# First norm's affine rows folded into the up weights, its token copy and the weight rounding moved to GpSimd, and all orders laid anew, in a one-core sandwich block

## The reference, cut to what matters

```
ln0(v)  = (v - mean) / sqrt(var + 1e-5)
ln(v)   = ln0(v) * g + b                      # the affine rows ln_g, ln_b
mlp(v)  = gelu(v @ w1 + b1) @ w2 + b2         # 128 -> 512 -> 128

# attention-like part, on u = ln0(x)
n  = ln(u)
W1, W2 = mlp_h1(n), mlp_h2(n)
t  = tril(W1 @ W2^T) @ n                      # per sequence of 256 tokens
x1 = u + ln(gelu(t))
x  = x + ln0(u + mlp_fm(ln(x1)))

# feed-forward part, on y = ln0(x), ternary weights, scales per output
h  = silu(y @ w1) * (y @ w2)
h  = gelu(gelu(h @ a) @ b)                    # 512 -> 512 -> 512
x  = x + ln0(h @ w3)
```

## Time and profile before

| | us |
|---|---|
| median of 3 runs | 365.95 |
| profiled execution: span from first to last instruction | 362.6 |
| median less this span | 3.35 |
| TensorE busy, share | 350.1, 97% |
| its weight loads busy | 289.2, 80% |
| VectorE | 319.9, 88% |
| ScalarE | 305.2, 84% |
| GpSimd | 147.2, 41% |

### The profile page before, as it was taken

How to read it: one execution, slowest core, us unless ns; L and a number is a source line. 1 busy time by engine, 2 the same in 40 slices (tenths; PEclk the granted TensorE clock), 3 DMA queues, 4 the chain that set the end, 5 groups by cost and what they waited for, 6 DMA issues and landing times.

```text
span 362.6 us, 6039 instructions
## 1 busy us (share of the span) xinstructions
PE 350.1 (97%) x1788; PEld 289.2 (80%) x1788; DVE 319.9 (88%) x954; ACT 305.2 (84%) x552; POOL 147.2 (41%) x213
## 2 busy tenths in 40 slices
PE   6989999999999999999999999999999999999993
PEld 5867687778888888888888888888888887788992
DVE  5889999999999999889989989998969998886936
ACT  5999999997779979988599888897799569959892
POOL 4168842860546052504750286003920174044411
PEclk9999999999999999999999999999999999999998
DMA  7507020000000000000010001000000001001111
GB/s 233 174 14 245 4 60 1 1 2 1 3 0 0 2 0 2 17 13 2 1 29 3 0 0 33 0 1 2 1 0 2 0 2 31 0 2 29 32 30 33
DMA packets 8804, 9.08 MB, mean 25 GB/s; under 512 B 577, under 2 KB 6722, under 8 KB 8770
## 3 DMA queue, kind: packets, MB, share of 16 engines
q1 hardware_dynamic: 8226, 8.41, 7.7%
q10 hardware_dynamic: 544, 0.26, 0.2%
HBM read 6.57 MB, written 2.10 MB: 24 GB/s over the span
## 4 chain that ended last, share of the span: by engine, by line
PE 67%; ACT 13%; DVE 10%; issue 5%; DMA 2%; POOL 1%; SPq 1%; POOLq 0%; DVEq 0%; ACTq 0%
PE bank L1224 8%; PE bank L1226 8%; PE bank L1240 6%; PE bank L1241 6%; PE bank L1123 4%; PE bank L1104 4%; PE bank L1108 4%; PE bank L1105 4%; PE bank L1120 4%; PE bank L1121 4%; PE bank L1206 4%; PE bank L1209 4%; ACT h_hidden_hi L510 3%; PE bank L1046 2%; ACT bank L515 2%
## 5 line engine op out<-in xcount | busy, mean ns | idle before, releaser
L715 DVE TENSOR_TENSOR ffn_gate_lo<-bank,ffn_gate_hi 128x512 fp32r<-128x512 f32 (+1 forms) x72 | 44.1, 626 | 6.0 <-ACT bank L584 4.9
L510 ACT ACTIVATE h_hidden_hi<-bank,cols 128x512 fp32r<-128x512 f32 x64 | 46.1, 760 | 3.5 <-PE bank L1108 3.2
L515 ACT ACTIVATE bank<-bank,cols 128x512 f32<-128x512 f32 x64 | 45.1, 739 | 0.3
L715 DVE TENSOR_TENSOR h_hidden_lo<-bank,h_hidden_hi 128x512 fp32r<-128x512 f32 x64 | 43.0, 681 | 2.5 <-ACT bank L515 2.5
L584 ACT ACTIVATE bank<-bank,cols 128x512 f32<-128x512 f32 (+1 forms) x72 | 43.7, 620 | 0.7
L1224 PE MATMUL bank<-ffn_gate_hi,ffn_w_hi 128*128 128x512 f32 (+1 forms) x108 | 40.5, 381 | 0.2 <-DVE ffn_gate_lo L715 0.2
L1226 PE MATMUL bank<-ffn_gate_lo,ffn_w_hi 128*128 128x512 f32 (+1 forms) x108 | 39.3, 370 | 0.2 <-DVE ffn_gate_lo L715 0.2
L578 ACT ACTIVATE ffn_h_hi<-bank,cols 128x512 fp32r<-128x512 f32 (+1 forms) x36 | 23.0, 646 | 13.5 <-PE bank L1226 8.3
L578 ACT ACTIVATE ffn_gate_hi<-bank,cols 128x512 fp32r<-128x512 f32 (+1 forms) x36 | 23.2, 647 | 10.6 <-PE bank L1226 8.3
L364 POOL TENSOR_TENSOR XR<-X,ln_x_r 128x512 f32<-128x512 f32 x8 | 8.3, 1042 | 53.6 <-DVE bank L861 53.4
L715 DVE TENSOR_TENSOR ffn_h_lo<-bank,ffn_h_hi 128x512 fp32r<-128x512 f32 (+1 forms) x36 | 22.0, 626 | 8.0 <-ACT bank L584 7.8
(11 more groups left out here) (164 smaller groups left out, 1132.3 us busy)
## 6 DMA issues: line engine op xcount, KB each, us to landing
raw<-ffn_w SPq DMA_DIRECT2D x5, 512.0 KB, 3.9
out<-X SPq DMA_DIRECT2D x7, 256.0 KB, 2.3
raw<-attn_w SPq DMA_DIRECT2D x6, 256.0 KB, 4.9
X<-x SPq DMA_DIRECT2D x3, 256.0 KB, 5.6
raw<-ffn_w SPq DMA_DIRECT2D x1, 256.0 KB, 3.2
X<-x ACTq DMA_DIRECT2D x1, 128.0 KB, 2.5
X<-x SPq DMA_DIRECT2D x1, 128.0 KB, 2.3
out<-X SPq DMA_DIRECT2D x1, 128.0 KB, 1.8
```

The source lines that it names most:

```text
L510: nc.scalar.activation(dst, bank(f"{L}u{j}", c)[:, :], ACT.Gelu, bias=bias_of(L, j)).then_inc(*hi[L].done(c, j))
L515: nc.scalar.activation(u[:, :], u[:, :], ACT.Gelu, bias=bias_of(L, j)).then_inc(*act2[L].done(c, j))
L715: return nc.vector.tensor_tensor(dst, whole, high.bitcast(f32), ALU.subtract)
```

## The change

1. `n_first` and `n_second` become one `n_norm(c)` on VectorE: four tensor_scalar, NF = (x - mean) * scale, with two per-partition scalars and no row. It waits for `n_lo(c - 1)` and for the scale.
2. The up weights of h1 and h2 are rounded with the scale column g, as those of fm were; `h_bias_product` (eight one-column matmuls with the column b, into a new bank group hb) and `h_bias_add` give the biases of h1 and h2. TensorE's transposes take the NF without the affine rows.
3. For the tokens GpSimd applies the rows in place, after the transposes: `n_gain(c)` and `n_shift(c)`, one 128x512 tensor_tensor each with a broadcast row; `n_high` waits for them, and `n_low` as before for `n_high`.
4. `ffn_w_hi` moves from ScalarE to GpSimd, as a tensor_copy into fp32r.
5. The bias b2 of fm comes by a DMA of one column into fm_b2, in place of a row, a tiny matmul and a copy; `fm_evict(0)` waits for it. SP issues it after chunk 2's x. SP waits for `h_b` too ahead of feed-forward piece 0, since the bias product reads raw.
6. TURNS and the lists of all four compute engines are laid anew. On TensorE `down_mm("h2", 3, 3)`, `down_mm("fm", 0, 1)` and `up_mm("fm", 3, 1)` move ahead of the branch.

```diff
-            def n_first(c):
+            def n_norm(c):
                 if c:
-                    dve.wait_ge(*nT.at(c - 1))
                     dve.wait_ge(*n_lo.at(c - 1))
-                else:
-                    dve.wait_ge(*rows_ready.at(0))
-                dve.wait_ge(*x_stats.at(c, 1))
-                for t in range(T):
-                    last = nc.vector.scalar_tensor_tensor(NF[:, t, :], X[:, c * T + t, :], mv("x", c)[:, t, 0:1], bc[:, R_G, :], ALU.subtract, ALU.mult)
-                last.then_inc(*n_v.done(c))
-
-            def n_second(c):
-                dve.wait_ge(*n_v.at(c))
                 dve.wait_ge(*x_scale.at(c, 1))
                 for t in range(T):
-                    nc.vector.scalar_tensor_tensor(NF[:, t, :], NF[:, t, :], x_s[:, t:t + 1], bc[:, R_B, :],
-                                                   ALU.mult, ALU.add).then_inc(*n_v_ready.done(c, t))
+                    nc.vector.tensor_scalar(NF[:, t, :], X[:, c * T + t, :], mv("x", c)[:, t, 0:1], x_s[:, t:t + 1],
+                                            ALU.subtract, ALU.mult).then_inc(*n_v_ready.done(c, t))
...
+            def n_gain(c):
+                if c == 0:
+                    pool.wait_ge(*rows_ready.at(0))
+                pool.wait_ge(*nT.at(c))
+                nc.gpsimd.tensor_tensor(NF[:, :, :], NF[:, :, :], row(R_G), ALU.mult).then_inc(*n_made.done(c, 0))
+
+            def n_shift(c):
+                pool.wait_ge(*n_made.at(c, 0))
+                nc.gpsimd.tensor_tensor(NF[:, :, :], NF[:, :, :], row(R_B), ALU.add).then_inc(*n_made.done(c, 1))
...
+            def ffn_w_hi(i):
+                c0, c1, at = F_PIECES[i]
+                pool.wait_ge(ffn_in[i], 16)
+                nc.gpsimd.tensor_copy(Fw[0][:, c0:c1], raw[:, at:at + c1 - c0]).then_inc(*ffn_hi.done(0, i))
...
             def attn_w_hi(i):
-                if i == PIECE["fmu"]:
+                if i in UP_PIECES:
...
+            def h_bias_product():
+                bank_free("hb", 0)
+                pe.wait_ge(cols_in, 16)
+                for L in ("h1", "h2"):
+                    pe.wait_ge(attn_in[PIECE[f"{L}u"]], 16)
+                    for j in range(J):
+                        w = ATTN[f"{L}u"] + j * P
+                        last = nc.tensor.matmul(bank("hb", 0)[:, C_B1[L] + j:C_B1[L] + j + 1], raw[:, w:w + P], cols[:, C_B:C_B + 1],
+                                                start=True, stop=True)
+                last.then_inc(*h_b.done(0))
...
+            def h_bias_add():
+                dve.wait_ge(*h_b.at(0))
+                nc.vector.tensor_tensor(h_bias[:, :], bank("hb", 0)[:, 0:2 * J], cols[:, 0:2 * J], ALU.add).then_inc(*h_b_added.done(0))
...
-            sp.dma_start(b2_row, rows[2:3, :]).then_inc(b2_in, 16)
             x_piece(1, 1, 2)
             for i in (3, 4, 5):
                 attn_piece(i)
             x_piece(2, 2, 3)
+            sp.dma_start(fm_b2[:, :], rows[2:3, :].rearrange("o d -> d o")).then_inc(b2_in, 16)
             for i in (0, 1):
                 sp.wait_ge(*attn_lo.at(0, 2 * i + 1))
+                if i == 0:
+                    sp.wait_ge(*h_b.at(0))
                 ffn_piece(i)
```

The first steps of GpSimd's order, before and after:

```diff
-            x_s_(0); n_low(0); x_s_(1); x_s_(2); lo_block(0); lo_block(1); x_r(0); xr_scale(0); lo_block(2); xr_b(0)
-            lo_block(3); n_low(1); t_r(0); x_r(1); lo_block(4); lo_block(5); x1_r(0); lo_block(6); lo_block(7); x_s_(3)
-            lo_block(8); n_low(2); t_r(1); xr_scale(1); xr_b(1); lo_block(9); o_r(0); x_r(2); x1_r(1); lo_block(10); y_r(0)
+            x_s_(0); n_gain(0); n_shift(0); n_low(0); ffn_w_hi(0); x_s_(1); lo_block(0); x_s_(2); x_r(0); lo_block(1)
+            xr_scale(0); n_gain(1); ffn_w_hi(1); ffn_w_hi(2); n_shift(1); lo_block(2); lo_block(3); n_low(1); x_r(1)
+            xr_b(0); t_r(0); lo_block(4); lo_block(5); ffn_w_hi(3); n_gain(2); x1_r(0); ffn_w_hi(4); x_s_(3); n_shift(2)
+            lo_block(6); lo_block(7); lo_block(8); ffn_w_hi(5); n_low(2); n_gain(3); lo_block(9); t_r(1); xr_scale(1)
+            xr_b(1); x_s_(4); o_r(0); lo_block(10); x1_r(1); n_shift(3); o_shift_(0); y_centre(0); y_r(0); y_scale(0)
```

And of VectorE's after, from chunk 2's pass to chunk 3's:

```diff
+            fm_bias_add(); up_lo("h1", 3, 1); x_st(4); t_st(0); n_norm(2); t_ag(0); up_lo("h2", 1, 1); t_gain(0)
+            nT_low(2); x1_sum(0); up_lo("h2", 2, 1); x1_st(0); x1_ag(0); up_lo("h2", 3, 1); down_lo("h1", 1)
+            up_lo("h1", 0, 2); x_ag(4); up_lo("h1", 1, 2); m_norm(0); down_lo("h2", 1); up_lo("h1", 2, 2)
+            up_lo("h2", 0, 2); mT_low(0); score_mask(0, 1); score_mask(1, 1); up_lo("h2", 1, 2); gate_constants()
+            score_lo(0, 1); score_lo(1, 1); up_lo("fm", 0, 0); up_lo("h2", 2, 2); up_lo("h1", 3, 2); up_lo("fm", 1, 0)
+            n_norm(3); up_lo("fm", 2, 0); t_st(1); up_lo("fm", 3, 0); t_ag(1); nT_low(3); t_gain(1); down_lo("h1", 2)
```

More of the change, by code:

```diff
@@ L88, in sandwich_block @@
     PIECE = {name: i for i, name in enumerate(ATTN)}
+    UP_PIECES = [PIECE[name] for name in ("h1u", "h2u", "fmu")]
     F_W1, F_W2, F_W3 = 0, DI, 2 * DI
@@ L430, in x_end @@
                 nc.gpsimd.tensor_tensor(xc(c), xc(c), FN[:, :, :], ALU.add).then_inc(*x_out.done(c))
-            x_s_(0); n_low(0); x_s_(1); x_s_(2); lo_block(0); lo_block(1); x_r(0); xr_scale(0); lo_block(2); xr_b(0)
-            lo_block(3); n_low(1); t_r(0); x_r(1); lo_block(4); lo_block(5); x1_r(0); lo_block(6); lo_block(7); x_s_(3)
-            lo_block(8); n_low(2); t_r(1); xr_scale(1); xr_b(1); lo_block(9); o_r(0); x_r(2); x1_r(1); lo_block(10); y_r(0)
-            y_centre(0); y_scale(0); o_shift_(0); n_low(3); x_s_(4); xr_scale(2); xr_b(2); o_r(1); t_r(2); x_r(3); x1_r(2)
@@ L436, in _ @@
-            y_r(1); y_centre(1); y_scale(1); o_shift_(1); x_s_(5); n_low(4); t_r(3); xr_scale(3); xr_b(3); x_r(4); f_r(0)
-            x1_r(3); o_r(2); y_centre(2); y_r(2); y_scale(2); x_end(0); f_r(1); n_low(5); xr_scale(4); t_r(4); o_shift_(2)
-            xr_b(4); o_r(3); x_r(5); x1_r(4); x_s_(6); y_r(3); y_centre(3); y_scale(3); o_shift_(3); x_end(1); x_s_(7)
-            xr_scale(5); o_r(4); n_low(6); xr_b(5); f_r(2); y_centre(4); y_r(4); o_shift_(4); t_r(5); y_scale(4); x_end(2)
-            x1_r(5); x_r(6); o_r(5); f_r(3); xr_scale(6); x_r(7); xr_b(6); n_low(7); y_r(5); t_r(6); y_centre(5); o_shift_(5)
@@ new lines, in _ @@
+            xr_b(0); t_r(0); lo_block(4); lo_block(5); ffn_w_hi(3); n_gain(2); x1_r(0); ffn_w_hi(4); x_s_(3); n_shift(2)
+            lo_block(6); lo_block(7); lo_block(8); ffn_w_hi(5); n_low(2); n_gain(3); lo_block(9); t_r(1); xr_scale(1)
+            xr_b(1); x_s_(4); o_r(0); lo_block(10); x1_r(1); n_shift(3); o_shift_(0); y_centre(0); y_r(0); y_scale(0)
+            n_low(3); x_r(2); xr_scale(2); n_gain(4); o_r(1); n_shift(4); xr_b(2); t_r(2); x_r(3); x_s_(5); x1_r(2)
+            y_r(1); y_centre(1); y_scale(1); n_low(4); t_r(3); o_shift_(1); xr_scale(3); xr_b(3); f_r(0); n_gain(5)
@@ new lines, in _ @@
+            o_r(2); x1_r(3); x_end(0); y_r(2); y_centre(2); o_shift_(2); x_r(4); y_scale(2); n_shift(5); f_r(1); t_r(4)
+            xr_scale(4); xr_b(4); x_end(1); o_r(3); x1_r(4); x_s_(6); n_low(5); y_r(3); x_r(5); y_centre(3); y_scale(3)
+            o_shift_(3); n_gain(6); o_r(4); x_s_(7); n_shift(6); xr_scale(5); f_r(2); t_r(5); y_r(4); xr_b(5); y_centre(4)
+            o_shift_(4); x_end(2); n_low(6); x1_r(5); y_scale(4); x_r(6); o_r(5); xr_scale(6); xr_b(6); t_r(6)
+            y_centre(5); n_gain(7); y_r(5); y_scale(5); x1_r(6); f_r(3); n_shift(7); x_end(3); x_r(7); o_shift_(5)
@@ L445, in _ @@
+            n_low(7); o_r(6); xr_scale(7); t_r(7); o_shift_(6); xr_b(7); y_centre(6); y_r(6); y_scale(6); x1_r(7); f_r(4)
+            o_r(7); x_end(4); y_centre(7); y_r(7); y_scale(7); f_r(5); x_end(5); o_shift_(7); f_r(6); x_shift(); x_end(6)
+            last_rstd(0); last_rstd(1)
         @block.scalar
@@ new lines, in _ @@
+            up_lo("h2", 3, 2); branch(0); up_lo("h1", 0, 3); o_st(0); up_lo("h1", 1, 3); down_lo("h2", 2); o_ag(0)
+            x1_sum(1); up_lo("h1", 2, 3); x1_st(1); x_branch(0); x1_ag(1); up_lo("h1", 3, 3); score_mask(0, 2)
+            up_lo("h2", 0, 3); lo_test(); m_norm(1); y_st(0); up_lo("h2", 1, 3); y_ag(0); score_lo(0, 2); mT_low(1)
+            up_lo("h2", 2, 3); score_mask(1, 2); lo_raise(); up_lo("h2", 3, 3); score_lo(1, 2); down_lo("h1", 3)
+            up_lo("fm", 0, 1); x_st(5); up_lo("fm", 1, 1); yT_low(0); n_norm(4); up_lo("fm", 2, 1); down_lo("h2", 3)
@@ new lines, in _ @@
+            gate_2(3, 3); up_lo("h1", 1, 6); branch(4); o_st(4); gate_lo(3, 3); o_ag(4); x_ag(7); up_lo("h2", 0, 6)
+            t_st(5); x_branch(4); f_st(2); up_lo("h1", 2, 6); layer_lo("a", 0, 3); f_ag(2); layer_lo("a", 1, 3)
+            layer_lo("a", 2, 3); y_st(4); t_ag(5); y_ag(4); t_gain(5); layer_lo("a", 3, 3); up_lo("h1", 3, 6); x1_sum(5)
+            x1_st(5); x1_ag(5); layer_lo("b", 0, 3); up_lo("h2", 1, 6); n_norm(7); m_norm(5); up_lo("h2", 2, 6)
```

(6 more changed lines are left out.)

559 lines of the change are left out of this document (272 added, 287 removed), and 45 rows, old and new, of the table TURNS.

## The result

The changed kernel takes 369.76 us (median of 7 runs, 367.33 to 370.62), beside 365.67 us for the kernel before (7 runs, 363.63 to 366.39): ratio 1.0103, 95% interval 1.0071 to 1.0135. The prediction was 363.1 us, with 0.16 on slower. Its profiled execution took 370.34 us with a span of 368.6.

What follows compares the result with a forecast made beforehand. VectorE and ScalarE were taken as the limits before 73 us. Terms -2.4 - 1.3 + 1.3 - 0.2 - 0.1 - 0.2 = -2.9 us gave 363.1 us; own range 361.5 to 364.9, 8-in-10 range 360.8 to 366.8.

Steps and rivals of the forecast that it cites:

- What bounds the kernel now: From 20 to 73 us VectorE and ScalarE limit TensorE; work taken from both is worth up to 6.2 us.
- the gauge: 0.831 us of weight loads per us, read from 80 to 280 us, taken as the rate of an unhindered TensorE stream.
- The start: Before the first matmuls: chunk 0's NF written in one pass, 0.2 us earlier (0 to 0.5); bias product put among waits.
- All this at nothing: At the start, bias product, b2 column load and h_bias_add cost nothing; without that cover, 0.95 us for the product.
- What GpSimd takes: Affine passes at 1.30 us each, six copies at 1.5 us per 1024 columns; VectorE waits 1.3 us for GpSimd.
- the first rival: At n_low(1) and n_low(2), copies near 2.5 us make GpSimd the limit: 366 to 369 us, chance 0.13.
- The walk's second place: Chunk 3: n_low(2) ends at 53.3 us, VectorE arrives at 52.0 and waits 1.3; n_norm(3) ends at 54.4.
- VectorE's norm passes: One pass of 1.1 us per chunk saves 1.2; chunks 2 and 3 give 2.4 us, the other chunks together 0.2.
- ScalarE's rounding: Six weight roundings, 7.0 us, leave ScalarE between 20 and 73 us, worth 1.3 us (0 to 2.7).
- The second rival: In chunks 1, 2, 3 n_norm and GpSimd shut each other out, some 3.6 us: 365.2 to 366.7 us, chance 0.12.
- The order of all engines: The new order across the kernel, including the chains after 280 us: 0, between 1.5 us lost and 0.7 won.
- Around the span: Outside the profiled span of 362.6 us lie 3.4 us by the median, which the change does not touch.

Runs made afterwards that it cites:

- h_bias last: The changed kernel with the tensor h_bias allocated behind all others, so every other tensor lies where it lay before: 364.26 us, 0.9976 of the kernel before.

## Why the prediction was wrong

*What bounds the kernel now.* Right in the main. TensorE's loss lay before 73 us, and work taken from ScalarE and VectorE there was worth time. With h_bias last, which leaves the rest of the change as it is, the loads from 20 to 73 us are these:

```profile
20.00:73.00 53.00, 50.83 (x260) 41.08 (x259) 50.10 (x150) 50.49 (x91) 43.70 (x48) 1.00 0.18 55
```

41.08 / 53 = 0.775 per us; 0.77 was predicted. By the gauge 6.2 us of loss became 53 - 41.08 / 0.831 = 3.6, a gain of 2.6. The kernel's gain was less, 365.63 - 364.26 = 1.4 us, half of the 2.9 forecast, since the start gave some of it back. Counting the matmuls of products in units of 512 columns, this kernel had started 37 of them at 20 us where the kernel before had 41, and 229.5 at 73 us where that had 225.5: 0.9 us lost at the start, 1.8 won in the stretch (the gauge says more, since it takes other loads along), 0.9 ahead at 73 us.

*The step that failed* is the prediction's first: "0.831 us of loads for each us is what this stream shows when nothing holds it up", carried over to the changed kernel as "still 0.83 after 80". The change moved the streamed operands by 32 bytes against the weights, and each 512-column matmul took 4 ns (mean) to 7 ns (median) more: the gauge after 80 us fell to 0.821, and the kernel took 3.6 to 4.6 us more, enough to turn the sign. With this term alone taken out (h_bias last) the kernel takes 364.26 us, inside the forecast's own range of 361.5 to 364.9. h_bias was in the diff, and the prediction costed its instructions and not its place. No row of the kernel before could have priced it. It could have been named as unknown, and a pad tried first.

*The start.* "Eight matmuls of one column, 0.95 us by the eight such instructions in the trace" miscounts: the row x8 was four matmuls of the code, so the product is sixteen instructions, 1.87 us at the upper level and 3.41 at the lower. "All this at nothing" was right in kind for the median, since leaving the product out saved 0.3 us; but by 20 us the kernel with h_bias last was 0.9 us behind and not 0.2 ahead.

*What GpSimd takes.* The copy was mis-sized, on the safe side: 1.04 us for 1024 columns when alone, not 1.5 (1.13 mean). So the first rival, by which the copies make GpSimd the limit, had no ground. By the Trainium skill, page GPSIMD Engine Reference, section "4.1 Engine selection", the estimate was 0.85; the trace stands between. The affine passes were right, 1.30 each. The walk's second place failed in another way: n_low(2) waited 1.96 us for ScalarE's n_high(2) and came at 56.25, and n_norm(3) ended at 58.70 us (56.06 with h_bias last), not at 54.4; before it ended at 56.8. The wait of 1.3 us that the sum subtracts for VectorE didn't show: VectorE, itself late, was idle for 0.14 us ahead of n_norm(3).

*VectorE's norm passes.* 1.12 us for four, 1.1 predicted. The totals that were to show it did so in part only: over the whole span VectorE is busy 3.0 us less (316.9) and not 9, ScalarE 2.6 less (302.6) and not 7, GpSimd 25.0 more (172.2) and not 29.

*ScalarE's rounding.* No run prices the 1.3 us by itself. Putting the roundings back costs 5 to 6 us in an order not laid for it, an upper bound.

*The second rival* was the right mechanism at the wrong places. That n_norm wasn't hit in chunks 2 and 3 (1.11 to 1.12 us, four parts without a gap) was the order's luck and not immunity: GpSimd ran nothing of full width beside it there, only its instructions of four columns or none. Where it did, the part was held, as in chunk 7 of the changed kernel, 1.06 us for the last part and not 0.34 (VectorE, then GpSimd):

```profile
228.23 1.83 DVE L789 TENSOR_SCALAR NF<-X,ln_x_mv,ln_x_s 128x128 f32<-128x128 f32 x4
228.84 1.14 POOL L423 TENSOR_TENSOR raw<-raw,ln_y_r 128x512 f32<-128x512 f32 x1
```

The argument against the rival, the plain 1.14 us of the old pass at 32.83, was no evidence either: GpSimd's n_low(1) had ended at 32.74 and GpSimd was idle until 34.34.

```profile
34.34 0.23 POOL L347 TENSOR_SCALAR ln_t_ve<-ln_t_mv 128x4 f32<-128x4 f32 x1 [1.61 <-DVE ln_t_mv L705]
```

The instructions whose delay reached TensorE were ones that read two SBUF operands, low weights and gate_coef. They cost the three stalls of 0.9 to 1.5 us, and parting them gave 1.85 us in one set and some 2.8 in the other. The prediction had the row for it: attn_w_lo beside n_low(0), 1.61 against 1.30, and argued from n_norm instead. The Trainium skill, page SBUF — State Buffer, section "Who interferes with whom", says that a VectorE instruction with two SBUF inputs contends with a GpSimd one that reads SBUF; the trace agrees, with 1.19 us against 0.17 for one of four columns.

*The order of all engines* was put at 0, between 1.5 lost and 0.7 won; from 280 to 340 us nothing of size was lost. The last stretch can't be judged: TensorE is at the half level for the last 2.7 us of the kernel before's trace and the last 6.1 of the changed one's (0.94 and 0.89 in the clock column), for 1.0 to 5.7 in the other variants, and the spans of one kernel differ by about 2 us between executions (362.6 and 364.4; 368.6 and 366.1).

*Around the span.* The 3.4 us are not what lies around it: every execution on record with both figures has 1.7 to 1.9 us more than its span. So the trace of the kernel before is of an execution of about 364.3 us and not of the median. The 363.1 us don't change by it, as the sum takes 2.9 off the median.
